# Attention and a routed feed-forward block on one core: the attention half written out without loops, in another order

## The chip, the core and the metric

One NeuronCore of a Trainium2 chip. TensorE (PE) multiplies matrices into PSUM, VectorE (DVE), ScalarE (ACT) and GpSimd (POOL) work on tiles in SBUF and PSUM, SyncE (SP) issues the DMAs. Each engine runs its own instruction list in order; the lists are tied together by semaphores. The metric is the time of one execution on the device in microseconds (us), less is better.

## The reference

x has 32 sequences of 256 tokens of width 128. One layer, two halves:

```python
x = x + attention(layernorm(x))      # 16 heads of 8, scale 1/sqrt(8)
#   allowed = (j <= i) & (j >= i - 128); softmax; out @ w_out.T + b_out
x = x + ffn(layernorm(x))            # 16 experts of 64, the best 4 of each token
#   (from the 2 best of 4 groups), silu(g) * u, weights * 2.5, and a shared expert
```

All in float32; the result is 32 x 256 x 128.

## The kernel before

The work goes in 16 steps of 512 tokens (two sequences, b = 0 and 1). Attention runs over all 16 steps and stores its result x1 in a scratch in DRAM; then the feed-forward half runs over 16 steps. In the attention half two steps are in flight: while step i is *prepared*, the step before it is *attended*.

Preparing (all names are functions of one engine's list): POOL and DVE make the LayerNorm (`statistics`, `layer_norm`), PE transposes it (`transpose_x`), ACT takes it out (`xT`); PE projects Q, K and V (`project_qk`, `project_v`). ACT rounds Q and K to float16 (`high_part`), DVE makes the remainder (`low_part`) and a spread form of Q (`qdiag`); SP stores both parts to DRAM and loads them back in another layout (`qstack`, `kstack`). ACT spreads V (`spread_v`). For the softmax a bound of each row is needed: `score_maxima(i, u)`, u = 0 to 7, computes rough scores on PE into two PSUM banks, DVE reduces them (`chunk_maxima`, `row_maxima`, four u per sequence), and SP takes these maxima through DRAM into `qstack` (`load_max`).

Attending: `scores(i, u)`, u = 0 to 9, five per sequence, writes two PSUM banks `ps_sc`; ACT takes the exponentials (`exps`) and PE may write the next scores when both are done. `attend` and `attend_tails` multiply by V, ACT takes the result (`take_att`), then `transpose_att` (PE), `normalise` (DVE), `transpose_attn` (PE), `take_attn` (ACT), `project_att` (PE) and `add_residual` (DVE) follow one another, for each of the two sequences. POOL's `residual` makes xres for it.

At the end of a body stand the tails, transpositions and projection of sequence 1, and the last maxima; the next body begins with `scores(i, 0)`, which waits for the loaded stacks and maxima. `last` attends step 15 while the weights of the feed-forward half are transposed.

Of the kernel before, what the change touches and what calls it, by code (L numbers as in the profile page):

```python
# [49 lines left out]
def build_block(nc, x, w_in, b_in, w_out, b_out, gate_w, e_bias, gate_proj, up_proj, down_proj,  # L50
# [39 lines left out]
    hl_d = nc.dram_tensor("qk_scratch", [2, P, 2, 2, TOK], FP16).ap()  # L90
# [3 lines left out]
    with ctx:  # L94
# [39 lines left out]
        qstack = [sb(f"qstack{p}", [P, G, TOK], FP16) for p in range(2)]  # L134
        kstack = [sb(f"kstack{p}", [P, G, TOK], FP16) for p in range(2)]
# [92 lines left out]
        w_loaded = sem("w_loaded")  # L228
        const_ready = sem("const_ready")
# [116 lines left out]

        @block.sync
        def _(sp):
            for p in range(2):
                sp.sem_inc(x1_stored[p], 16)  # L350
                sp.sem_inc(stored[p], 16)
# [3 lines left out]
            for n in range(2):  # L355
                sp.dma_start(bqk[:, n:n + 1], b_in[n * P:(n + 1) * P].unsqueeze(1)).then_inc(w_loaded, 16)
            sp.dma_start(bv[:, :], b_in[2 * P:3 * P].unsqueeze(1)).then_inc(w_loaded, 16)
            sp.dma_start(boB[:, :], b_out.partition_broadcast(P)).then_inc(w_loaded, 16)
            sp.dma_start(xin[1][:, :, :], x_t[1]).then_inc(x_loaded[1], 16)
            gu = wgu_raw[:, :, :]  # L360
            for n, w in enumerate((gate_proj, up_proj)):
                sp.dma_start(gu[:, n * NP:(n + 1) * NP, :],
                             w.rearrange("e i h -> (e i) h").rearrange("(n p) h -> p n h", p=P)).then_inc(ffn_loaded, 16)
            sp.dma_start(wsh_raw[0:I, :], sh_gate).then_inc(ffn_loaded, 16)
            sp.dma_start(wsh_raw[I:2 * I, :], sh_up).then_inc(ffn_loaded, 16)
            sp.dma_start(wr_raw[:, :], gate_w).then_inc(ffn_loaded, 16)
            sp.dma_start(wd_raw[:, :, :], down_proj.rearrange("e h i -> h e i")).then_inc(ffn_loaded, 16)
            sp.dma_start(wds_raw[:, :], sh_down).then_inc(ffn_loaded, 16)
            sp.dma_start(bias[:, :], e_bias.partition_broadcast(P)).then_inc(ffn_loaded, 16)
            sp.wait_ge(buffers_ready, 1)  # L370
# [5 lines left out]
            def store_split(i):  # L376

                p = i.parity

                if i.begun:  # L380
                    sp.wait_ge(sc_full, i.lag(2 * UNITS, 0))
                sp.sem_inc(sp_passed, 1)
                for part, ready in ((0, high_ready), (1, low_ready)):
                    sp.wait_ge(ready, i.count(2, 2))
                    sp.dma_start(hl_d[p, :, part], hl[:, part, :, :]).then_inc(split_stored[p], 16)
                sp.wait_ge(split_stored[p], i.half(32, 32))
                for stack, n, parts in ((qstack[p], 0, (0, 1, 0)), (kstack[p], 1, (0, 0, 1))):
                    for t, part in enumerate(parts):
                        for r in range(C):
                            sp.dma_start(stack[32 * r + HD * t:32 * r + HD * t + HD, :, :],  # L390
                                         hl_d[p, :, part, n, :].rearrange("(g r d) t -> r d g t", g=G, r=C)[r]
                                         ).then_inc(qk_loaded[p], 16)

            def load_max(i, b):

                if i.begun:
                    sp.wait_ge(max_loaded[b], i.count(16, 0))
                sp.sem_inc(sp_passed, 1)
                sp.wait_ge(rowmax_ready, i.count(2, b + 1))
                sp.dma_start(mx_d[b], rowmaxT[b][:, :]).then_inc(max_stored[b], 16)  # L400
                sp.wait_ge(max_stored[b], i.count(16, 16))
                sp.dma_start(qstack[i.parity][3 * HD:P:32, :, b * S:(b + 1) * S],
                             mx_d[b].rearrange("(c g n) q -> c g (n q)", c=C, g=G)
                             ).then_inc(max_loaded[b], 16)

            def load_x(i):
                src = x_t[row(i, 2)]
                sp.wait_ge(xres_ready, i.count(1, 1))
                sp.dma_start(xin[i.parity][:, :, :], src).then_inc(x_loaded[i.parity], 16)

            def store_x1(i):

                p = 1 - i.parity
                dst = x1_d[row(i, -1)]
                sp.wait_ge(x1_ready, i.lag(2, 2))
                sp.dma_start(dst, x1[p].rearrange("p t e -> p (t e)")).then_inc(x1_stored[p], 16)

            def first(i):
                store_split(i)
                load_x(i)  # L420
                for b in range(2):
                    load_max(i, b)
# [8 lines left out]

            def body(i):
                store_split(i)
                if not (i.j is None and i.c + 2 >= STEPS):
                    load_x(i)
                else:

                    sp.wait_ge(xres_ready, i.count(1, 1))
                    load_x1(Step(None, 0), i.c + 2 - STEPS)
                for b in range(2):  # L440
# [1202 lines left out]
```

## Time and profile before

| | |
|---|---|
| median of 3 runs | 1018.19 us (1014.93 to 1023.9) |
| profiled execution | 1021.8 us, its span 1019.8 us |
| busy PE / DVE / ACT / POOL | 840.5 / 594.7 / 368.4 / 169.6 us |
| mean granted clock of PE | 0.857 of full |
| attention half, to about | 622 us |
| DMA queue of SP | 54768 packets, 44.51 MB |
| queue of instructions | 78 packets, 1.28 MB |

The page shows the span in 40 slices; up to the 24th PE is 6 to 8 tenths busy at a clock of 6 to 9 tenths, after that 9 and 9. In the rows below, a row of the order of time gives start, duration, engine, line, operation, what is written from what is read, and in brackets the idle time of that engine before it with what ended it; neighbouring instructions of one kind are merged (x8).

### The profile page before, as it was taken

To read this page: it belongs to the slowest core of one execution; us is meant where nothing else is said; L and a number is where in the kernel's file an instruction comes from. 1 tells how busy PE (TensorE), PEld (TensorE's weight loads), DVE (VectorE), ACT (ScalarE), POOL (GpSimd) and SP (SyncE) were. 2 spreads that over 40 slices of the span, in tenths; PEclk is the share of its full clock that TensorE was granted. 3 is DMA by queue.
4 is the path that set the end of the run, shared out by engine and by line. 5 is a ranking of instruction groups with operands and counts; after the bars stand their busy time and mean duration, and the time that the engine had idled before them with its cause. 6 is when DMAs were issued, how large, how long until landed. Compare 5 with 4: busy or idle time off the path is not lost. (4 is left out here: it accounts for less than half of the span.)

```text
span 1019.8 us, 25253 instructions
## 1 busy us (share of the span) xinstructions
PE 840.5 (82%) x8978; PEld 525.6 (52%) x9009; DVE 594.7 (58%) x1874; ACT 368.4 (36%) x709; POOL 169.6 (17%) x289
## 2 busy tenths in 40 slices
PE   3677787777686786777777778999999999999998
PEld 2454444444354453444544446656666666666665
DVE  6545445454554454464455436777777777777774
ACT  2234434343442443444345262332323332323332
POOL 5401101100110110111011102222121222222200
PEclk9667776797797787797768777999999999999999
DMA  4323123213313412331132101110110110100000
GB/s 126 67 36 76 46 32 75 54 54 46 72 42 40 75 54 36 64 69 46 38 76 55 33 1 52 32 31 31 31 31 31 31 31 31 31 31 31 21 21 21
DMA packets 54859, 45.88 MB, mean 45 GB/s; under 512 B 12513, under 2 KB 44529, under 8 KB 54769
## 3 DMA queue, kind: packets, MB, share of 16 engines
q1 hardware_dynamic: 54768, 44.51, 19.9%
q8 instruction: 78, 1.28, 0.6%
q14 instruction: 13, 0.10, 0.0%
HBM read 27.44 MB, written 17.04 MB: 44 GB/s over the span
## 5 line engine op out<-in xcount | busy, mean ns | idle before, releaser
L687 ACT ACTIVATE probs<-ps_sc 128x512 f32<-128x512 f32 x256 | 139.0, 595 | 155.3 <-PE ps_sc L1280 155.2
L868 DVE TENSOR_REDUCE chunkmax<-ps_max 128x16 f32<-128x512 f32 (+1 forms) x256 | 155.0, 647 | 62.5 <-PE ps_max L1244 62.5
L766 ACT ACTIVATE spare<-ps_max 128x512 f32<-128x512 f32 x144 | 85.9, 597 | 212.3 <-PE ps_max L1515 171.2
L1262 PE MATMUL ps_max<-hl,qdiag 32*128 32x160 f16 (+4 forms) x1024 | 59.7, 248 | 84.6 <-DVE chunkmax L868 80.3
L1531 PE MATMUL ps_c<-spare,wd 128*128 128x512 f32 x256 | 125.4, 592 | 0.0
L1302 PE MATMUL ps_sc<-qstack,kstack 32*64 32x192 f16 (+2 forms) x2048 | 75.5, 263 | 44.5 <-ACT probs L687 23.6
L1326 PE MATMUL ps_att<-probs,vdiag 128*32 128x192 f32 (+1 forms) x1536 | 96.6, 403 | 4.8 <-ACT probs L687 4.7
L1092 DVE TENSOR_TENSOR spare<-spare,ps_sc 128x512 f32<-128x512 f32 x128 | 87.2, 681 | 21.7 <-ACT spare L766 11.7
L1262 PEld LDWEIGHTS ps_max<-hl,qdiag 32*128 32x128 f16 x1024 | 39.2, 107 | 111.5 <-DVE chunkmax L868 96.4
L1100 DVE TENSOR_TENSOR spare<-spare,ps_att 128x512 f32<-128x512 f32 x128 | 87.2, 681 | 10.7 <-PE ps_att L1523 4.1
L1302 PEld LDWEIGHTS ps_sc<-qstack,kstack 32*64 32x64 f16 x2048 | 42.4, 120 | 88.3 <-ACT probs L687 43.5
L1513 PE MATMUL ps_max<-xh,whigh 128*128 128x512 f32 x144 | 79.4, 552 | 0.1
L554 POOL TENSOR_TENSOR xres<-xin,cvec 128x512 f32<-128x512 f32 x16 | 20.8, 1298 | 347.1 <-DVE x L914 343.3
L902 DVE RECIPROCAL rden<-ps_b 128x32 f32<-128x32 f32 x32 | 11.4, 358 | 114.9 <-PE ps_b L1356 114.9
L1326 PEld LDWEIGHTS ps_att<-probs,vdiag 128*32 128x32 f32 x1536 | 54.6, 137 | 32.1 <-issue 7.4
L528 POOL TENSOR_TENSOR veps<-meanvar,eps 128x4 f32<-128x4 f32 x32 | 7.6, 236 | 326.2 <-DVE meanvar L841 326.2
L1531 PEld LDWEIGHTS ps_c<-spare,wd 128*128 128x128 f32 x256 | 48.4, 189 | 23.7 <-issue 11.5
L1280 PE MATMUL ps_sc<-edges,repeat 64*128 64x192 bf16 (+2 forms) x576 | 57.5, 276 | 0.0
L1515 PE MATMUL ps_max<-xh,wlow 128*128 128x512 f32 x144 | 57.5, 399 | 0.0
L1514 PE MATMUL ps_max<-xl,whigh 128*128 128x512 f32 x144 | 57.2, 397 | 0.0
L698 ACT COPY attTn<-ps_c 128x256 f32<-128x256 f32 x32 | 11.9, 372 | 123.1 <-PE ps_c L1364 123.1
L914 DVE TENSOR_TENSOR x<-ps_c,xres 128x256 f32<-128x256 f32 x32 | 13.6, 425 | 67.5 <-PE ps_c L1370 67.5
(156 smaller groups left out, 1430.3 us busy)
## 6 DMA issues: line engine op xcount, KB each, us to landing
qk_scratch<-hl SPq DMA_DIRECT2D x32, 256.0 KB, 2.3
qstack<-qk_scratch SPq DMA_DIRECT2D x192, 32.0 KB
kstack<-qk_scratch SPq DMA_DIRECT2D x192, 32.0 KB
xin<-in_L_attn_x_dram SPq DMA_DIRECT2D x16, 256.0 KB, 5.4
x_scratch<-x SPq DMA_DIRECT2D x16, 256.0 KB, 2.7
xin<-x_scratch SPq DMA_DIRECT2D x16, 256.0 KB, 3.0
xres<-x_scratch SPq DMA_DIRECT2D x16, 256.0 KB, 2.7
out_dram<-result SPq DMA_DIRECT2D x16, 256.0 KB, 2.5
```

What stands on the lines that cost most here:

```text
L687: nc.scalar.activation(dst[:, :], ps_sc[s][:, 0:dst.shape[1]], ACT.Exp, scale=SCALE).then_inc(probs_ready, 1)
L766: nc.scalar.activation(silu[slot][rows, :], ps_max[slot][rows, :], ACT.Silu).then_inc(silu_ready, 1)
L868: nc.vector.tensor_reduce(chunkmax[:, 2 * pair + m, at:at + CHUNKS[h]], ps_max[m][:, 0:BANK_COLS[h]].rearrange("p (n k) -> p n k", k=KB), ...
L1092: tt(gated[slot][:, :], silu[slot][:, :], ps_sc[slot][:, :], ALU.mult).then_inc(gated_ready, 1)
L1100: tt(inter[p % 3][:, :], gated[(k.parity + p) % 2][:, :], ps_att[:, :], ALU.mult).then_inc(inter_ready, 1)
L1262: mm(ps_max[m][:, at:at + width], qdiag[rows, b * NB + n, :, :].rearrange("p c k -> p (c k)"), hl[rows, 0, 1, b * S + key0:b * S + key0 + ...
L1280: return mm(ps_sc[s][:, cols].rearrange("p (n k) -> p n k", n=n), repeat2[rows, :, :].rearrange("p e k -> p (e k)"), edges2[rows, edge, :] ...
L1302: mm(dst, kstack[p][rows, jj, q0:q0 + TB], qstack[p][rows, jj, q0:q0 + QCOLS[m]].rearrange("p (n k) -> p n k", k=TB), start=(at == 0), sto ...
L1326: last = mm(ps_att[32 * x:32 * x + 32, half * S + TB * m:half * S + TB * m + QCOLS[m]].rearrange("p (n k) -> p n k", k=TB), vdiag[p][:, (b ...
L1513: mm(bank[slot][:, :], whigh[:, n, :], xh[q][:, :], start=True, stop=False)
L1515: last = mm(bank[slot][:, :], wlow[:, n, :], xh[q][:, :], start=False, stop=True)
L1531: last = mm(ps_c[:, :], wd[:, p, :], inter[p % 3][:, :], start=(p == 0), stop=False)
```

## The change

The whole attention half is written out for all 16 steps (the feed-forward half keeps its loops). A body i now attends `now = i - 1` and prepares `prep = i`, and three things cross its seam: the second sequence of the step before (`transpose_att(now - 1, 1)`, `normalise`, `transpose_attn`, `project_att`, `add_residual`) runs between the first scores of the next body, and so do the eighth `score_maxima` and the second `row_maxima` of the step just prepared. V is projected by four matmuls, each of 128 tokens by all 128 columns, and `spread_v` picks the 64-token halves out with four copies. Q and K lie in one tile `qkstack`; the DRAM scratch has the layout of the stacks, so it is stored with 8 DMAs and loaded with 12. In the prologue, the weights, the small biases and the output bias have a semaphore each, the zeroing of the buffers of parity 1 comes later, and the feed-forward weights are loaded at the end of body 1.

```diff
-    hl_d = nc.dram_tensor("qk_scratch", [2, P, 2, 2, TOK], FP16).ap()
+    hl_d = nc.dram_tensor("qk_scratch", [2, 32, 4, G, TOK], FP16).ap()
...
 # SP
+            for i in BODIES:
+                load_max(i - 1, 1)
+                store_x1(i - 2)
+                load_x(i + 1)
                 store_split(i)
+                load_stacks(i)
+                load_max(i, 0)
+                if i == 1:
+                    load_ffn_weights()
...
+                    for g in range(G):
+                        sp.dma_start(hl_d[p][:, part::2, g, :], hl[32 * g:32 * g + 32, part, :, :]
+                                     ).then_inc(split_stored[p], 16)
...
+                    for t, parts in enumerate((slice(0, 4, 2), slice(0, 4, 3), slice(1, 3, 1))):
+                        rows = slice(32 * r + HD * t, 32 * r + HD * t + HD)
+                        sp.dma_start(qkstack[p][rows, :, :, :], src[r][:, parts, :, :]).then_inc(qk_loaded[p], 16)
...
 # POOL
+            for i in range(STEPS):
+                residual(i)
+                layer_norm(Step(None, i + 1))
+                if i == 0:
+                    other_constants()
...
 # ACT
+                now, prep = i - 1, i
+                exps(now, 0)
+                take_attn(now - 1, 1)
+                exps(now, 1)
+                high_part(prep, 0)
+                exps(now, 2)
+                high_part(prep, 1)
+                exps(now, 3)
+                exps(now, 4)
+                spread_v(prep)
+                exps(now, 5)
+                take_att(now, 0)
+                exps(now, 6)
+                exps(now, 7)
+                take_attn(now, 0)
+                exps(now, 8)
+                exps(now, 9)
+                transpose_out(prep + 1)
+                take_att(now, 1)
...
 # PE
-                for n in range(part * NKB // 2, (part + 1) * NKB // 2):
-                    for e in range(2):
-                        last = mm(ps_a[TB * e:TB * e + TB, n * TB:(n + 1) * TB].rearrange("p (n d) -> p n d", d=HD),
-                                  xT[:, n * TB:(n + 1) * TB], wv[:, e], start=True, stop=True,
-                                  tile_position=(0, TB * e))
+                mm(ps_a[:, t * P:(t + 1) * P], xT[:, t * P:(t + 1) * P], wT[:, 2, :], start=True, stop=True
+                   ).then_inc(v_done, 1)
...
+                now, prep = i - 1, i
+                scores(now, 0)
+                transpose_att(now - 1, 1)
+                project_v(prep, 0)
+                score_maxima(now, 7)
+                scores(now, 1)
+                transpose_attn(now - 1, 1)
+                project_qk(prep, 0)
+                project_att(now - 1, 1)
+                scores(now, 2)
+                project_v(prep, 3)
+                project_qk(prep, 1)
+                scores(now, 3)
+                project_v(prep, 1)
...
+                score_maxima(prep, 0)
+                attend(now, 0, 0)
+                scores(now, 4)
+                project_v(prep, 2)
+                score_maxima(prep, 1)
+                scores(now, 5)
+                attend(now, 0, 1)
+                score_maxima(prep, 2)
+                attend_tails(now, 0)
+                scores(now, 6)
+                transpose_att(now, 0)
+                score_maxima(prep, 3)
+                scores(now, 7)
+                transpose_attn(now, 0)
+                attend(now, 1, 0)
+                scores(now, 8)
+                score_maxima(prep, 4)
+                transpose_x(prep + 1)
+                project_att(now, 0)
+                scores(now, 9)
+                score_maxima(prep, 5)
+                attend(now, 1, 1)
+                attend_tails(now, 1)
+                score_maxima(prep, 6)
```

TensorE at the seam of two steps. Before, inside the loop body (L1342 is `attend_tails`, L1262 and L1244 the maxima, L1356 `transpose_att`, L1364 `transpose_attn`, L1370 `project_att`, L1302 and L1280 the scores, L1218 Q and K):

```order
L1342 MATMUL ps_att<-tails,vdiag 32x64 x8
...
L1356 MATMUL ps_b<-ident,attT 128x128 x4
L1226 MATMUL ps_a<-wT,xT 64x64 x4
L1364 MATMUL ps_c<-ident,att 128x128 x2
L1370 MATMUL ps_c<-wT,attTn 128x128 x2
```

After (L1391 the tails, L1305 and L1286 the maxima, L1347 and L1323 the scores, L1408, L1422, L1432 the three pieces of sequence 1, L1271 a piece of V, L1264 Q and K):

```order
L1391 MATMUL ps_att<-tails,vdiag 32x64 x8
...
L1347 MATMUL ps_sc<-qkstack 64x3x64 x8
...
L1408 MATMUL ps_b<-ident,attT 128x128 x4
L1271 MATMUL ps_a<-wT,xT 128x128
...
L1347 MATMUL ps_sc<-qkstack 64x3x64 x8
...
L1422 MATMUL ps_c<-ident,att 128x128 x2
L1264 MATMUL ps_b<-xT,wT 128x512
L1432 MATMUL ps_c<-wT,attTn 128x128 x2
L1347 MATMUL ps_sc<-qkstack 64x3x64 x8
```

The three pieces that followed one another directly now have scores, maxima or a projection between them.

VectorE around the row maxima of sequence 0. Before (L868 `chunk_maxima`, L902 and L905 `normalise`, L885 to L896 `row_maxima`):

```order
L868 TENSOR_REDUCE chunkmax<-ps_max 128x14
L902 RECIPROCAL rden<-ps_b 128x32
L905 TENSOR_TENSOR att<-ps_b,rden 128x256
L885 TENSOR_REDUCE rowmax<-chunkmax 128x4x3
L885 TENSOR_REDUCE rowmax<-chunkmax 128x4 x5
```

After (L897, L934 and L937, L916 to L926):

```order
L897 TENSOR_REDUCE chunkmax<-ps_max 128x16 x2
L934 RECIPROCAL rden<-ps_b 128x32
L937 TENSOR_TENSOR att<-ps_b,rden 128x256
L897 TENSOR_REDUCE chunkmax<-ps_max 128x14 x2
L916 TENSOR_REDUCE rowmax<-chunkmax 128x4x3
L916 TENSOR_REDUCE rowmax<-chunkmax 128x4 x5
```

`normalise` stood with the row maxima behind the fourth pair of reductions; now it stands in front of that pair.

SP in one step. Before (L385 the split, L390 the stacks, L409 x, L400 and L402 the maxima, L416 x1):

```order
L385 DMA qk_scratch<-hl 128x1024 x2
L390 DMA qstack<-qk_scratch 8x4x512 x12
L390 DMA kstack<-qk_scratch 8x4x512 x12
L409 DMA xin<-in_L_attn_x_dram 128x4x128
L400 DMA max_scratch<-rowmaxT 128x32
L402 DMA qstack<-max_scratch 4x4x256
```

After, the same operations of a step (L419 and L421 the maxima, L442 x1, L432 x, L397 the split, L411 the stacks, in all 12):

```order
L419 DMA max_scratch<-rowmaxT 128x32
L421 DMA qkstack<-max_scratch 4x4x256
L442 DMA x_scratch<-x_0 128x512
L432 DMA xin<-in_L_attn_x_dram 128x4x128
L397 DMA qk_scratch<-hl 64x1x512 x8
L411 DMA qkstack<-qk_scratch 8x2x2048 x2
L411 DMA qkstack<-qk_scratch 8x4096
```

The maxima of sequence 1, x1 and x come ahead of the split and the stacks, and those are other pieces: 8 stores and 12 loads.

## Rows read from the trace of the kernel before

**Rows 1.** Windows: span, busy us (instructions) per engine, PE clock, DMA share, GB/s.

```profile
39.50:578.00 538.50, 406.06 (x6942) 250.02 (x6944) 266.32 (x773) 219.16 (x434) 67.24 (x74) 0.78 0.28 54
...
626.10:1019.80 393.70, 382.56 (x1479) 240.16 (x1507) 283.09 (x961) 120.85 (x221) 74.91 (x146) 1.00 0.09 28
...
284.80:300.00 15.20, 13.14 (x242) 8.39 (x240) 8.72 (x26) 8.74 (x17) 1.30 (x1) 1.00 0.07 22
...
312.10:322.30 10.20, 9.97 (x129) 6.21 (x133) 2.83 (x6) 3.75 (x8) 0.00 (x0) 0.50 0.43 50
...
303.60:312.00 8.40, 4.90 (x133) 3.16 (x128) 5.13 (x16) 3.52 (x8) 0.33 (x1) 1.00 0.47 70
```

**Rows 2.** Order of time: first scores of the first and of the sixteenth step.

```profile
39.52 0.64 PE L1302 MATMUL ps_sc<-qstack,kstack 32*64 32x192 f16 x12
...
577.96 0.41 PE L1302 MATMUL ps_sc<-qstack,kstack 32*64 32x192 f16 x12
```

**Rows 3.** TensorE's waits in the 15 steps: total us, times, longest.

```profile
PE ps_max L1262 <- DVE chunkmax L868: 69.1, 45, 3.1
...
PE ps_sc L1302 <- issue: 19.8, 6, 3.6
```

**Rows 4.** Order of time: the two kinds of 3 us holes on TensorE.

```profile
312.21 0.55 PE L1262 MATMUL ps_max<-hl,qdiag 32*128 32x160 f16 x8 [3.04 <-DVE chunkmax L868]
...
330.38 0.64 PE L1302 MATMUL ps_sc<-qstack,kstack 32*64 32x192 f16 x12 [3.06 <-issue]
```

**Rows 5.** Order of time, TensorE alone, a stretch at full clock.

```profile
288.33 1.08 PE L1326 MATMUL ps_att<-probs,vdiag 128*32 128x192 f32 x24
...
289.33 0.45 PE L1226 MATMUL ps_a<-wT,xT 128*64 128x64 f32 x8
...
289.72 0.43 PE L1342 MATMUL ps_att<-tails,vdiag 128*32 128x64 f32 x16
...
290.46 0.37 PE L1262 MATMUL ps_max<-hl,qdiag 32*128 32x160 f16 x8
...
290.86 0.66 PE L1356 MATMUL ps_b<-ident,attT 128*128 128x128 f32 x4
...
291.44 0.45 PE L1226 MATMUL ps_a<-wT,xT 128*64 128x64 f32 x8
...
293.96 0.41 PE L1302 MATMUL ps_sc<-qstack,kstack 32*64 32x192 f16 x12
...
294.64 1.10 PE L1218 MATMUL ps_b<-xT,wT 128*128 128x512 f32 x2
...
296.53 0.41 PE L1302 MATMUL ps_sc<-qstack,kstack 32*64 32x192 f16 x12
```

**Rows 6.** Order of time: one round of scores and exponentials.

```profile
306.10 0.41 PE L1302 MATMUL ps_sc<-qstack,kstack 32*64 32x192 f16 x12
...
306.79 1.08 ACT L687 ACTIVATE probs<-ps_sc 128x512 f32<-128x512 f32 x2 [1.69 <-PE ps_sc L1280]
...
307.93 0.41 PE L1302 MATMUL ps_sc<-qstack,kstack 32*64 32x192 f16 x12 [0.37 <-ACT probs L687]
```

**Rows 7.** Order of time: the spreading of Q beside POOL, and without it.

```profile
17.20 2.17 DVE L855 TENSOR_SCALAR qdiag<-hl,headrow 128x512 f16<-128x512 f16 x4
...
17.37 1.33 POOL L554 TENSOR_TENSOR xres<-xin,cvec 128x512 f32<-128x512 f32 x1 [3.51 <-DVE cvec L934]
...
334.17 1.14 DVE L855 TENSOR_SCALAR qdiag<-hl,headrow 128x512 f16<-128x512 f16 x4 [4.72 <-ACT hl L666]
```

**Rows 8.** Order of time: twelve load issues on SP.

```profile
303.69 4.07 SPq L390 DMA_DIRECT2D qstack<-qk_scratch  x12
```

**Rows 9.** SP's waits over the span: total us, times, longest.

```profile
SPq L402 <- DMA max_scratch<-rowmaxT: 67.0, 32, 5.1
```

**Rows 10.** Order of time: prologue, the load that held SP, the weight transposes.

```profile
6.16 4.19 SPq L364 DMA_DIRECT2D wsh_raw<-L_ffn_shared_gate_w_dram  x1
...
8.99 1.11 PE L1380 MATMUL ps_b<-ident,wraw 128*128 128x128 f32 x4 [8.99 <-DMA boB<-in_L_attn_b_out_dram]
```

More of the change, by code:

```diff
@@ L344, in steps, with after, valid @@
             last(Step(None, STEPS))
+        def after(engine, semaphore, value):
+            if value > 0:
+                engine.wait_ge(semaphore, value)
+        def valid(d, last=STEPS - 1):
+            return 0 <= d <= last
+        BODIES = range(-1, STEPS + 2)
         @block.sync
@@ L424, in load_x1 @@
+            for p in range(2):
+                sp.wait_ge(x1_stored[p], 16 * (STEPS // 2))
             def load_x1(k, d):
@@ L574, in _, with other_constants @@
             pool.wait_ge(cvec_ready, 1)
[L576 to L581 removed]
+            def other_constants():
                 nc.gpsimd.memset(repeat2[:, :, :], 0.0).then_inc(const_ready, 1)
@@ new lines, in body @@
+            def body(i):
+                now, prep = i - 1, i
+                normalise(now - 1, 1)
+                chunk_maxima(now, 7)
+                row_maxima(now, 1)
+                add_residual(now - 1, 1)
+                spread_q(prep)
+                low_part(prep, 0)
+                low_part(prep, 1)
+                chunk_maxima(prep, 0)
+                chunk_maxima(prep, 1)
+                statistics(Step(None, prep + 1))
+                chunk_maxima(prep, 2)
+                normalise(now, 0)
+                chunk_maxima(prep, 3)
+                row_maxima(prep, 0)
+                if i == 0:
+                    clear(1)
+                chunk_maxima(prep, 4)
+                chunk_maxima(prep, 5)
+                add_residual(now, 0)
+                chunk_maxima(prep, 6)
@@ L1115, in add_y, with last @@
                                         xres[p][:, :, :], ALU.add).then_inc(result_ready, 1)
-            def last(i):
+            def last(now):
                 k = Step(None, 0)
+                normalise(now - 1, 1)
+                chunk_maxima(now, 7)
+                row_maxima(now, 1)
+                add_residual(now - 1, 1)
                 dve.wait_ge(ffn_loaded, 16 * 8)
@@ L1541, in transpose_y, with last @@
                 last.then_inc(y_tr_done, 1)
-            def last(i):
+            def last(now):
+                scores(now, 0)
+                transpose_att(now - 1, 1)
+                score_maxima(now, 7)
+                scores(now, 1)
+                transpose_attn(now - 1, 1)
+                project_att(now - 1, 1)
+                scores(now, 2)
                 pe.wait_ge(ffn_loaded, 16 * 8)
```

650 lines of the change are left out of this document (285 added, 365 removed).

## Prediction

> **What bounds the kernel now.** I read the stretches first, then the waits of TensorE, then one stretch in order of time, always asking which wait ends last.
>
> The feed-forward half, from 626.1 us on, has TensorE 97% busy at a clock of 1.00 [rows 1]. The change does not touch it, so it stays, 394 us. The attention half is where everything is decided: from the first `scores` (39.52 us) to the first `scores` of `last` (577.96 us) lie 15 steps [rows 2], 538.4 / 15 = 35.9 us each. In them TensorE is busy 406 of 538 us, at a mean clock of 0.78; VectorE is busy 266 / 15 = 17.8 us a step and ScalarE 219 / 15 = 14.6 us [rows 1]. No engine is full. Three things fill the step:
>
> - Waits of TensorE for `chunkmax`, 69.1 us in all, and "issue" waits of 3.1 us at the loop's back edge, 19.8 us in 6 [rows 3]. One row of each is in [rows 4]: the `score_maxima` behind row maxima and normalisation on VectorE (3.04 us), and `scores(i, 0)` after the branch (3.06 us); in the seam inside the loop body, where no branch is, that wait does not occur (the `scores` at 293.96 in [rows 5] begins without one).
> - The clock. A clock of 0.78 made of 1.0 and 0.5 means 44% of the stretch at 1.2 GHz, 237 us. The stretch after the 3 us wait, 312.10 to 322.30, runs at 0.50 with TensorE 9.97 of 10.20 us busy; 284.80 to 300.00, with only short waits, runs at 1.00 [rows 1]. So a 3 us hole costs itself and then a stretch at half level, in which TensorE is the bound.
> - The serial end of a step: tails, `transpose_att`, normalise, `transpose_attn`, copy, `project_att` with no scores between them; from `attend` at 288.33 to the next scores at 293.96 pass 5.6 us [rows 5] in which the exponentials stand still.
>
> **The change, part by part.** The sum is made against the profiled execution, 1021.8 us; the median shown is 1018.2.
>
> *TensorE's work in a step at full level*, start to start in [rows 5]: four `attend` at 1.00, eight `score_maxima` at 0.40, `transpose_att` 0.58 twice, Q and K projections 1.89 together, eight full `scores` up to 0.68 and two short ones (estimate 0.46), tails 0.43 twice as durations, the value projection 4 x 0.39, and for the transposes of x, of the normalised heads and the output projections 0.6, 2 x 0.4 and 2 x 0.65 (estimates from the four transposes at 0.58). Sum 21.7 us. The 128-token value matmuls: 16 that stream 64 columns become 4 that stream 128, half as many columns in all. Bounds: no gain (1.6 us) and half of it (0.8 us); I take 1.2, nearest to four pieces like a transpose and its load. So 21.3 us of TensorE at full level; at half level twice that, 42 us.
>
> *ScalarE's chain.* One pair of exponentials takes 1.08 us and the whole round scores, exponentials, next scores takes 1.83 us (306.10 to 307.93) [rows 6]. Eight rounds of 1.83 and two short ones of 1.3 (estimate) are 17.2 us. Of ScalarE's 14.6 us a step about 10 are exponentials; the other 4.6 (`take_attn`, `high_part`, `spread_v`, the copies) partly fall into its waits for scores and partly lengthen a round; I add 3, so about 20.5 us. `spread_v` becomes four copies of half the size for two: under 0.5 us more, inside those 3.
>
> *VectorE.* The same instructions, 17.8 us, plus short semaphore waits: 19 to 20 us. New order: the last `chunk_maxima` and `row_maxima` of a step move behind the seam, `normalise` between two maxima, and between maxima 3 and 4 TensorE now has scores 7, scores 8 and a whole `attend` (about 2.4 us) to do while VectorE makes the row maxima. That is the cover of the old 3.04 us hole; I leave 0.5 us of it.
>
> *The seam.* `transpose_att`, `transpose_attn` and `project_att` of half 1 now stand between scores 0, 1 and 2 of the next step, and each latency to VectorE or ScalarE is covered by a scores piece. 5.6 us shrink to the 2.2 us of TensorE work that is in them. Following all four engines through one body at these durations I get about 21 to 21.5 us: every engine nearly full, TensorE first.
>
> *What is added on top.* (1) `residual` is released by `add_residual(now-1, 1)` and now runs beside `spread_q`. In the prologue of the kernel before those two overlap and `qdiag` takes 2.17 us for its four pieces; alone it takes 1.14 [rows 7]. Cost 0 to 1.0 us a step, I take 1.0, VectorE having no slack. The Trainium skill (SBUF — State Buffer, Who interferes with whom) says that a VectorE operation in a two-port mode and a GpSimd one exclude each other for the whole instruction; by it the full 1.0 is paid, against this change, as I took it. (2) SP: the split is stored in 8 issues for 2, loaded in 12 for 24. Twelve issues take 4.07 us [rows 8], 0.34 each, so 20 issues cost 6.8 us for 8.8 before. With the last `low_part` at about 8 us into the body, stores land at 13, load issues end at 17, row maxima (ready at about 17) go out then and come back behind the loads at 21 to 22, when scores 0 wants them. The bound from below is nothing; from above the worst wait of L402 before, 5.1 us for the store, against its mean of 67.0 / 32 = 2.1 [rows 9]. I take 0.7 us. (3) Some stretches at half level remain after holes, in the hardest places (after scores 5 and at the seam). Bounds: none, and as much as now. 10 us at half level do 5 us of work; I take 1.5 us a step, 3 us at half level in 24.5.
>
> Step after: 21.3 + 1.0 + 0.7 + 1.5 = **24.5 us**, gain 11.4 a step, 15 x 11.4 = **171 us**. The back edges' 19.8 us are inside it.
>
> *Once.* Prologue: the weight transposes waited for the last bias load, until 8.99 us [rows 10]; their own two loads are among the first three issued, so they can go some 3 us earlier, but the LayerNorm of x bounds the next piece: between 0 and -6, I take -4. The feed-forward weights' loads, one of which held SP for 4.19 us [rows 10], move from the prologue into body 1, ahead of row maxima, x load and split stores of step 2: between 0 and +12, I take +5. The last part gets half 1 of step 14 and the eighth maxima: +2 to +4, I take +3. Together +4.
>
> 1021.8 - 171 + 4 = 854.8 in a profiled execution; its 3.6 us above the median are half undone: **853 us**.
>
> **The rivals.**
>
> *A. The DMA chain sets the step (0.25).* If stores of 1 KB pieces and loads are no quicker in landing than before, the chain low part, store, load, row maxima, scores 0 takes about 28 us: loads issued from 14, landed at 25 (the 768 KB came in at 70 GB/s, so over 11 us, before [rows 1]), maxima there at 28. Then, with the holes' half-level stretches, 28 to 31 us a step: 1021.8 - 15 x 7.9 + 4 = 907, up to 952. For it: the chain is linear and starts late; against it: the loads are half as many, with longer pieces. The Trainium skill (DMA: Bandwidth & Descriptors, Why a DMA increments its semaphore by 16 and not by 1) says that a copy spreads over the largest number of engines up to 16 that divides its outer dimension: 8 rows would use 8 engines, before and after. By that alone the loads gain nothing but their piece length; no row here shows the engine numbers.
>
> *B. Everything fits (0.10).* No collision, no half level: 21.5 us, 1021.8 - 216 + 4 = 810.
>
> *C. The straight program starves TensorE (0.04), slower.* The loop is gone, 15 bodies are fetched in sequence. A step has (6942 + 6944) / 15 = 926 TensorE instructions; if fetching stalled like the back edge (3.06 us [rows 4]) after every 200 of them, 5 times a step, a step would be 24.5 + 15.3 = 39.8 us: 1021.8 + 15 x 3.9 + 4 = 1084. From four stalls a step on it loses. Against it: inside a loop body of two steps, 284.80 to 300.00 ran 242 matmuls at full level [rows 1], with no such wait. The Trainium skill (Runtime: NRT & Kernel Launch, Instruction fetch mechanics) says that sequential fetch is autonomous and only a taken branch stalls it; by it C does not happen.
>
> *D. Most of the gain is given back (0.06).* Small holes everywhere keep the clock at its present 0.78: TensorE needs 21.3 / 0.78 = 27 us plus the holes of today without the two big kinds, about 33 to 35: 982 to 1012.
>
> The forecast itself: 0.55.
>
> **Numbers.** 853 us. The forecast's own range, with period 23 to 26.5: 830 to 885. To leave out no more than 2 in 10 the range takes in most of A and half of B: 815 to 945. What a measurement tells from no change is about 1%. Faster by over 1%: forecast, A, B and nearly all of D, 0.94; within 1%: 0.02; slower: 0.04.
>
> **What would show it.** In the profile after: attention ending near 460 us and not 622; TensorE 85% or more busy there, clock 0.93 or more; no issue wait of 3 us before `scores`; waits for `chunkmax` under 20 us in all; `qdiag` at twice its mean; TensorE's wait for `max_loaded` before scores 0 under 1 us. A wait of several us there says A, a clock below 0.85 with many small waits D, issue waits inside a body C. I am wrong if VectorE or ScalarE hold a chain that the walk through one body missed.

## The result, and the profile after

The changed kernel takes **949.71 us** (median of 4 runs, 948.31 to 956.55) against 1017.39 of the kernel before beside it: ratio 0.934, 95% interval 0.928 to 0.940. It is faster, as forecast, but the forecast was 853 us and its range ended at 945. The profiled execution took 948.31 us, its span is 946.6. In what follows a ratio rests on fast runs alone, which leaves out one run of e2 (1683.42 us) and two of e2b (886.69 and 885.51).

Windows of the changed kernel (columns as in [rows 1]): the 15 steps and the last part, the feed-forward half, one body while TensorE works, the hole behind it (a stretch in which TensorE does nothing), and the start of the next body.

```profile
36.11:546.60 510.49, 376.87 (x6976) 251.50 (x6972) 291.56 (x850) 239.96 (x502) 73.81 (x85) 0.81 0.28 61
546.60:946.60 400.00, 388.60 (x1504) 244.68 (x1532) 287.02 (x970) 124.95 (x228) 74.92 (x146) 0.99 0.10 30
292.00:315.00 23.00, 22.65 (x440) 15.25 (x440) 17.19 (x51) 14.68 (x31) 4.67 (x5) 0.89 0.29 67
314.90:323.60 8.70, 0.00 (x0) 0.01 (x1) 1.29 (x2) 0.11 (x1) 0.00 (x0) 0.65 0.32 47
...
323.60:329.60 6.00, 5.98 (x58) 3.95 (x59) 2.91 (x12) 2.35 (x5) 0.00 (x0) 0.50 0.01 3
```

The body itself is as dense as hoped: 22.65 of 23.00 us busy. Then TensorE does nothing for 8.7 us, and the next body begins at half level. First scores of the first and of the sixteenth step, against [rows 2]:

```profile
36.11 0.64 PE L1347 MATMUL ps_sc<-qkstack 32*64 32x192 f16 x12
...
506.92 0.64 PE L1347 MATMUL ps_sc<-qkstack 32*64 32x192 f16 x12 [8.96 <-issue]
```

(506.92 - 36.11) / 15 = **31.4 us a step**, for 35.9 before and 24.5 forecast. TensorE's waits over the span, against [rows 3]:

```profile
PE ps_sc L1347 <- issue: 119.3, 15, 9.6
PE ps_max L1305 <- DVE chunkmax L897: 13.3, 6, 6.4
```

The waits for `chunkmax` are nearly gone (69.1 to 13.3). One new wait has come, once a step, 119.3 / 15 = 8.0 us. "issue" names no releaser, so who ended it has to be read from the neighbours. SP's queue through this body, in order of time, gives it:

```profile
297.40 0.34 SPq L419 DMA_DIRECT2D max_scratch<-rowmaxT  x1
298.82 0.54 SPq L421 DMA_DIRECT2D qkstack<-max_scratch  x1
299.41 0.45 SPq L442 DMA_DIRECT2D x_scratch<-x  x1
299.89 0.43 SPq L432 DMA_DIRECT2D xin<-in_L_attn_x_dram  x1
300.94 5.54 SPq L397 DMA_DIRECT2D qk_scratch<-hl  x8
309.01 6.29 SPq L411 DMA_DIRECT2D qkstack<-qk_scratch  x12
315.41 0.35 SPq L419 DMA_DIRECT2D max_scratch<-rowmaxT  x1
321.56 0.54 SPq L421 DMA_DIRECT2D qkstack<-max_scratch  x1
```

And TensorE and VectorE at its two ends:

```profile
310.51 0.21 DVE L926 STREAM_TRANSPOSE rowmaxT<-rowmax 128x32 f16<-128x32 f16 x1
```

```profile
314.62 0.26 PE L1286 MATMUL ps_max<-edges,repeat 32*128 32x192 bf16 x4
323.62 0.64 PE L1347 MATMUL ps_sc<-qkstack 32*64 32x192 f16 x12 [8.74 <-issue]
```

The row maxima are ready at 310.7. SP is still issuing the 12 stack loads and takes them up at 315.41, just when TensorE runs out of work. Their 8 KB store, which comes back in 1.4 us when it is alone (297.40 to 298.82), now comes back after 6.15 us (315.41 to 321.56), behind 768 KB of stack loads in the same queue. Their load leaves then, and 2.06 us later scores 0 starts. The windows behind the last load issue (315.30) show what the store waited for: the stack loads' data were still moving, until 320.0.

```profile
315.30:320.00 4.70, 0.00 (x0) 0.00 (x0) 0.90 (x2) 0.00 (x0) 0.00 (x0) 0.74 0.52 77
320.00:321.50 1.50, 0.00 (x0) 0.00 (x0) 0.00 (x0) 0.00 (x0) 0.00 (x0) 0.50 0.02 1
```

So the loads take 6.29 us to issue, but 11.0 us until their data are in (309.01 to 320.0; 768 KB, about 70 GB/s). SP's waits over the span fit (before: 67.0 in [rows 9]):

```profile
SPq L421 <- DMA max_scratch<-rowmaxT: 97.4, 32, 6.1
```

### The profile page after: what moved, and what is told of

The parts are those of the page before. It is cut to its first block and busy times, and to the rows that moved or that the text cites. A ratio compares the mean times of both kernels' runs of the same rounds, so it can differ in the third digit from the quotient of the medians.

```text
span 946.6 us, 23269 instructions
## 1 busy us (share of the span) xinstructions
PE 778.6 (82%) x8594; PEld 505.3 (53%) x8625; DVE 602.4 (64%) x1874; ACT 371.0 (39%) x741; POOL 170.3 (18%) x289
## 5 line engine op out<-in xcount | busy, mean ns | idle before, releaser
L897 DVE TENSOR_REDUCE chunkmax<-ps_max 128x16 f32<-128x512 f32 (+1 forms) x256 | 155.5, 649 | 38.3 <-PE ps_max L1286 38.2
L1347 PE MATMUL ps_sc<-qkstack 32*64 32x192 f16 (+2 forms) x2048 | 71.7, 252 | 121.7 <-issue 119.3
L1347 PEld LDWEIGHTS ps_sc<-qkstack 32*64 32x64 f16 x2048 | 41.0, 114 | 154.1 <-issue 129.8
L934 DVE RECIPROCAL rden<-ps_b 128x32 f32<-128x32 f32 x32 | 11.4, 357 | 137.4 <-PE ps_b L1408 137.3
L1373 PE MATMUL ps_att<-probs,vdiag 128*32 128x192 f32 (+1 forms) x1536 | 70.6, 318 | 0.0
L1305 PE MATMUL ps_max<-hl,qdiag 32*128 32x160 f16 (+4 forms) x1024 | 53.1, 227 | 15.3 <-DVE chunkmax L897 13.3
L1323 PE MATMUL ps_sc<-edges,repeat 64*128 64x192 bf16 (+2 forms) x576 | 54.1, 262 | 0.0
L1305 PEld LDWEIGHTS ps_max<-hl,qdiag 32*128 32x128 f16 x1024 | 34.2, 98 | 35.9 <-DVE chunkmax L897 20.6
L1373 PEld LDWEIGHTS ps_att<-probs,vdiag 128*32 128x32 f32 x1536 | 44.0, 111 | 16.2 <-issue 3.2
L1552 PE MATMUL ps_sc<-xl,whigh 128*128 128x512 f32 x128 | 51.0, 398 | 0.0
L1553 PE MATMUL ps_sc<-xh,wlow 128*128 128x512 f32 x128 | 50.5, 395 | 0.0
```

Of the source, the lines that this page charges most:

```text
L897: nc.vector.tensor_reduce(chunkmax[:, 2 * pair + m, at:at + CHUNKS[h]], ps_max[m][:, 0:BANK_COLS[h]].rearrange("p (n k) -> p n k", k=KB), ...
L1305: mm(ps_max[m][:, at:at + width], qdiag[rows, b * NB + n, :, :].rearrange("p c k -> p (c k)"), hl[rows, 0, 1, b * S + key0:b * S + key0 + ...
L1347: mm(dst, qkstack[p][rows, 1, jj, q0:q0 + TB], qkstack[p][rows, 0, jj, q0:q0 + QCOLS[m]].rearrange("p (n k) -> p n k", k=TB), start=(at == ...
L1373: last = mm(ps_att[32 * x:32 * x + 32, half * S + TB * m:half * S + TB * m + QCOLS[m]].rearrange("p (n k) -> p n k", k=TB), vdiag[p][:, (b ...
L1552: mm(bank[slot][:, :], whigh[:, n, :], xl[q][:, :], start=False, stop=False)
L1553: last = mm(bank[slot][:, :], wlow[:, n, :], xh[q][:, :], start=False, stop=True)
```

## The experiments

All ratios are against the kernel before on the same chip. "Step" is (first scores of step 15 - first scores of step 0) / 15, read from each trace as above.

### Is it the stack loads, and what about them?

**e1**: 3 loads in place of 12. The rows of a stack are interleaved, so that one DMA brings all 32 rows of a kind, 256 KB.

```diff
-                for r in range(C):
-                    for t, parts in enumerate((slice(0, 4, 2), slice(0, 4, 3), slice(1, 3, 1))):
-                        rows = slice(32 * r + HD * t, 32 * r + HD * t + HD)
-                        sp.dma_start(qkstack[p][rows, :, :, :], src[r][:, parts, :, :]).then_inc(qk_loaded[p], 16)
+                for t, parts in enumerate((slice(0, 4, 2), slice(0, 4, 3), slice(1, 3, 1))):
+                    sp.dma_start(qkstack[p][t:P:4, :, :, :], hl_d[p][:, parts, :, :]).then_inc(qk_loaded[p], 16)
```

> The kernel after, but the 32 rows of a row group of the stacks are interleaved (row 32r + 4d + t instead of 32r + 8t + d), so that one load can fill every fourth of the 128 rows: 3 loads of 32 rows (256 KB each) for 12 of 8 rows. Same data, same result. In the kernel after, TensorE ends its body 23 us after it began and then waits 8.0 us on average for stacks and maxima. Theory W (the loads of 8 rows are slow in themselves, 768 KB in some 9.5 us, and everything behind them waits): data in about 5 us, first scores 5 to 7 us earlier a step, 949.7 - 15 x 6 = 860 (840 to 875). Rival I (what counts is only the time that SP issues, 6.3 us for 12 loads): issue falls to under 2 us, gain about 4 us a step, 890. Rival Q (the maxima's own round trip through DRAM is the long part): gain under 2 us a step, 920 to 950.

**e2**: the interleaved rows, but still 12 loads of 8 rows (`slice(32 * r + t, 32 * r + 32, 4)`).

> As e1_wide_loads in the rows' layout (every fourth row), but still 12 loads of 8 rows. It separates what the eight rows of a load lie next to from how many there are. Theory W by number of rows: no change against the kernel after, 940 to 955. If writing eight neighbouring rows were the slow part: 860 to 900. Rival I and Q: no change.

**e3**: the maxima's store and load issued by GpSimd, ahead of and behind its LayerNorm, instead of by SP.

> The kernel after, but the store and the load of the row maxima are issued by GpSimd and not by SP, so they do not stand behind SP's 12 stack loads. Theory W: the stacks themselves land about 19.5 us after their body's high part, some 3 us before the maxima do now, so the wait of TensorE shrinks from 8.0 to about 4.5 to 5.5 us and not further: 949.7 - 15 x 3 = 905 (890 to 925). Rival Q: the wait goes nearly, 840 to 860. Against both: a GpSimd that is late with the LayerNorm of the next step, because it waits for the store, would make it no faster, 945 or more.

e1: **846.92 us**, ratio 0.832 (0.827 to 0.837), step 24.50. e2: 932.37 (median of the three), 0.913 (0.909 to 0.916), step 30.41. e3: 925.61, 0.907 (0.904 to 0.910), step 29.83. TensorE's wait before the scores in e1, and its SP queue in one body:

```profile
PE ps_sc L1344 <- issue: 32.6, 15, 3.8
```

```profile
266.86 5.48 SPq L397 DMA_DIRECT2D qk_scratch<-hl  x8
273.97 1.87 SPq L408 DMA_DIRECT2D qkstack<-qk_scratch  x3
276.70 0.32 SPq L416 DMA_DIRECT2D max_scratch<-rowmaxT  x1
279.87 0.56 SPq L418 DMA_DIRECT2D qkstack<-max_scratch  x1
```

The same 768 KB in three DMAs, and the wait falls from 8.0 to 2.2 us a step: the loads are the cause of most of it. e1 lies in the range of its theory W. In e3, just over the range of its theory W, the maxima pass the loads by, and TensorE still waits, now for the stacks themselves, with a releaser named:

```profile
PE ps_sc L1348 <- DMA qkstack<-qk_scratch: 83.3, 14, 8.1
```

So the maxima's detour behind the loads is the smaller share: 31.4 - 29.8 = 1.6 us a step (the prologue of e3 is 4 us longer).

Two readings of e1 were left: it has fewer loads, and wider ones (32 rows). **e7** parts them: 12 loads of 32 rows, 64 KB each.

```diff
+                for t, xs in enumerate(((0, 2), (0, 3), (1, 2))):
+                    for n, x in enumerate(xs):
+                        for g in (0, 2):
+                            sp.dma_start(qkstack[p][t:P:4, n, g:g + 2, :], hl_d[p][:, x, g:g + 2, :]).then_inc(qk_loaded[p], 16)
```

> As e1_wide_loads, 32 rows in each load, but 12 loads of 64 KB (pieces of 2 KB) for 3 of 256 KB: the same number and size of loads as in the kernel after. Theory W (the number of rows in a load is what counts): data in some 5 us, SP's issue time of about 6 us is then the longer part, 855 to 880. Rival I (12 issues are what makes it slow): 935 to 955, as after and e2_spread_rows.

**e2b**: 6 loads of 16 rows.

> The change with 6 stack loads of 16 rows and 4 KB a row instead of 12 of 8 rows (between e1, 3 loads of 32 rows, and e2 and e7, 12 loads of either 8 or 32 rows). Theory I (SyncE pays for each load by number, up to 0.7 us an issue): issue time near the straight line between 1.9 us for 3 and 8.5 us for 12, so about 4.1 us for 6; TensorE's wait before the first scores 2 us longer than e1's 2.2, step near 26.5 us, time 865 to 885. Rival theory W (rows and engines in a load decide, with 32 rows as the good case): 16 rows lie near 8 rows' 8 us of wait, 905 to 930. Rival S (only the first few issues are cheap, a queue's depth of some 6 to 8 outstanding loads has to be filled first): 6 still cost little, 845 to 855.

e7: 933.85, 0.915 (0.911 to 0.920), step 30.25. e2b: 881.01 and 868.20, against 1017.99 (no interval was formed), step 26.79 in the first of them, which was profiled. The loads' issue in each:

```profile
295.68 8.46 SPq L410 DMA_DIRECT2D qkstack<-qk_scratch  x12
```

```profile
295.60 4.19 SPq L410 DMA_DIRECT2D qkstack<-qk_scratch  x6
```

My theory W, that the rows of a load decide, fell: 12 loads of 32 rows (933.85) are as slow as 12 of 8 rows four apart (e2, 932.37). So e1's time lay in W's range for another reason. With the rows interleaved the number of loads decides, through the issue: 3, 6 and 12 loads (e1, e2b, e7) take 1.87, 4.19 and 8.46 us of SP, 0.62 to 0.71 us each, and give steps of 24.5, 26.8 and 30.3 us, 0.76 and 0.58 us of the step for each load more. A load costs 0.70 us in six as in twelve, against rival S of e2b.

The changed kernel itself is another case, and its 12 loads of 8 neighbouring rows must not be put in that row. They issue in 6.29 us, faster than e7's, but their data go on for 4.7 us behind the last issue, at a DMA share of 0.52. In e2 (first line) and e7 (second) the data end 1.3 us behind the last issue:

```profile
306.86:308.20 1.34, 0.00 (x0) 0.00 (x0) 0.00 (x0) 0.00 (x0) 0.00 (x0) 0.73 0.36 101
304.14:305.50 1.36, 0.00 (x0) 0.00 (x0) 0.00 (x0) 0.00 (x0) 0.00 (x0) 0.59 0.46 105
```

From the first load issue to the last data are 11.0 us in the changed kernel, 9.8 in e2 and e7, and 4.5 in e1 (273.97 to 278.5). What ends this time is the moving of the data in the first and the issuing in e2 and e7; nearly equal steps hide two limits. Why eight neighbouring rows move more slowly than eight rows four apart is open.

**e8** made the same loads wide in the kernel before (6 for 24):

> The kernel before with the interleaved rows and 6 loads of 32 rows for 24 of 8. There no wait of TensorE for stacks or maxima is in the trace, so the loads have slack: no change, 1012 to 1022, if the reading is right that the slow loads were hidden in steps of 36 us and only the short step of the new order uncovers them. If they already cost something there: under 1010.

1018.33 against 1018.67, ratio 0.999 (0.996 to 1.002). There the loads were covered, as expected; it is the change that puts them on the path.

### What is left in e1?

**e5**: e1 with `residual` behind the LayerNorm on GpSimd, so that it no longer meets `spread_q`.

> e1_wide_loads, with GpSimd's residual behind the LayerNorm of the next step and no longer in front of it, so that it does not run beside the spreading of Q on VectorE. In e1 the four pieces of qdiag take 578 ns each in the steps, 349 in the kernel before. Theory C (VectorE waits out GpSimd, and it has no slack): qdiag back to 349, 0.9 us a step, 847 - 14 = 833 (830 to 840). Theory N (VectorE has slack there): qdiag back to 349 and the time unchanged, 843 to 851.

847.59, 0.831 (0.828 to 0.834): no gain. By line and form, busy us and mean ns, of e1 and then of e5 (both 36 to 405 us), and then of the kernel before (39.5 to 578 us):

```profile
L872 DVE TENSOR_SCALAR qdiag<-hl,headrow 128x512 f16<-128x512 f16 x60 | 31.1, 578 | 2.4 <-ACT hl L677 2.4
L919 DVE TENSOR_SCALAR rowmax<-rowmax 128x32 f16<-128x32 f32 x30 | 5.4, 181 | 1.0
```

```profile
L875 DVE TENSOR_SCALAR qdiag<-hl,headrow 128x512 f16<-128x512 f16 x60 | 17.1, 348 | 1.9 <-ACT hl L680 1.7
L922 DVE TENSOR_SCALAR rowmax<-rowmax 128x32 f16<-128x32 f32 x30 | 16.0, 532 | 1.0
```

```profile
L855 DVE TENSOR_SCALAR qdiag<-hl,headrow 128x512 f16<-128x512 f16 x60 | 17.1, 349 | 37.7 <-ACT hl L666 37.7
L891 DVE TENSOR_SCALAR rowmax<-rowmax 128x32 f16<-128x32 f32 x29 | 15.2, 524 | 1.0
```

`qdiag` was freed (578 to 348 ns), but another operation met GpSimd instead (`rowmax`, 181 to 532 ns), so VectorE gained only 36.5 - 33.1 = 3.4 us in 15 steps, and e5 is no test of what the collision costs. The kernel before had the same collision at `rowmax` (524 ns): the change moved it to `qdiag` and added 36.5 - 32.3 = 4.2 us, 0.3 a step. The Trainium skill (SBUF — State Buffer, Who interferes with whom) calls the shared port an exclusive lock; the trace agrees with these lengths. What the collision costs at most is seen in e13b below, where `qdiag` still takes 562 ns and TensorE is 96% busy.

**e10**: e1 with the old value projection (16 matmuls of 64 by 64, two copies), to price the new one.

> e1_wide_loads with the value projection of before: 16 matmuls of 64 columns and two spreading copies for 4 of 128 columns and four copies. It prices that part of the change. The prediction took 0.4 us a step from TensorE, 6 us in all: 853 (848 to 860). If TensorE does not set the step there: 845 to 850; if the two copies fewer on ScalarE count more: under 845.

861.24, 0.843 (0.839 to 0.848), step 25.43 for 24.50, just over the expected range: the new projection with its copies is worth 0.9 us a step there.

**e11**: e1 with 2 split stores of 128 rows in place of 8 of 32, into the same scratch layout. **e1p** and **e12**: e1 and e11 with the maxima issued by GpSimd.

```diff
-                    for g in range(G):
-                        sp.dma_start(hl_d[p][:, part::2, g, :], hl[32 * g:32 * g + 32, part, :, :]
-                                     ).then_inc(split_stored[p], 16)
+                    sp.dma_start(hl_d[p][:, part::2, :, :].rearrange("r x g t -> g r x t"), hl[:, part, :, :]
+                                 ).then_inc(split_stored[p], 16)
```

> e1 (3 wide stack loads) with 2 split stores of all 128 rows in place of 8 of 32 rows; same bytes and same pieces of 1 KB. Theory I (cost by the number of DMAs): the stores' issue falls from 5.5 us to the 2.4 us that 2 stores took before the change; the loads leave 3 us earlier, TensorE's 2.2 us before the scores go; step 22.3 to 23.0, time 815 to 828. Rival D (issue time goes with the number of pieces in a DMA, not with the number of DMAs): the 2 stores take 5 us too, and the time stays at 845 to 850.

> e1 (3 wide stack loads) with the maxima's store and load issued by GpSimd instead of SyncE. In e1 the store of the second half's maxima leaves at 276.70 and its load at 279.87, 3.17 us later, against 1.4 for the first half's; TensorE waits 2.2 us a step at the first scores. Theory I: what is left of the wait is the maxima's round queued behind the stack loads on SyncE's queue: on another queue the load leaves 1.5 us earlier, the stacks themselves then end the wait; step 23.0 to 24.0, time 825 to 842. Rival: what is left is the chain of 8 split stores (5.5 us) and the stack loads' own landing, so nothing changes, 845 to 852; or GpSimd, in order, stands 3 us in the two rounds ahead of LayerNorm, and the time goes up to 855 to 870.

> e11 with the maxima's rounds issued by GpSimd as well. Theory I: after e11 nothing is left to gain from SyncE's queue but what sits behind the stack loads, within 1% of e11, 812 to 828: TensorE has the bound then, at 21.3 to 22.5 us a step. Rival: GpSimd's own rounds delay LayerNorm and it is 1 to 2% slower than e11.

e11: 876.48, 0.860 (0.858 to 0.863). e1p: 863.09, 0.845 (0.840 to 0.850). e12: 861.25, 0.845 (0.842 to 0.849). All three are slower than e1; both theories of e11 missed, and so did theory I of e1p and e12. Moving the maxima to GpSimd made e1 16 us slower (e1p) and e11 15 us faster (e12). The queue of e11, its waits, and the window in which its stores land:

```profile
287.23 1.67 SPq L396 DMA_DIRECT2D qk_scratch<-hl  x2
296.43 1.86 SPq L407 DMA_DIRECT2D qkstack<-qk_scratch  x3
```

```profile
SPq L405 <- DMA qk_scratch<-hl: 122.1, 16, 8.3
```

```profile
288.90:296.40 7.50, 7.24 (x182) 4.82 (x174) 6.41 (x24) 5.94 (x14) 3.28 (x4) 1.00 0.24 71
```

Issuing fell to 1.67 us as expected, but landing rose to 122.1 / 16 = 7.6 us, at 71 GB/s with a DMA share of 0.24. The store's outer dimension in the scratch is the 4 head groups. The Trainium skill (DMA: Bandwidth & Descriptors, Why a DMA increments its semaphore by 16 and not by 1) says that a DMA runs on the largest number of engines up to 16 that divides the outer dimension of both sides, so on 4 here; a share of 0.24 fits 4 of 16. The rule alone does not tell e2 from the changed kernel, both with 8 rows in a load: the share of 0.52 behind the changed kernel's last issue fits 8 of 16, while in e2, where the issuing is the limit, it is 0.36.

Why e1p lost those 16 us I did not settle. It lies in the range of its rival that GpSimd stands in the maxima's rounds ahead of LayerNorm (855 to 870), but no row shows that. Its first scores come 4.2 us later (40.47 for 36.23), once; TensorE's wait stays mostly an "issue" one.

**e13b** tests the outer dimension of the stores: the scratch laid out by its 128 rows as before the change, 2 stores with those rows outside, and 6 loads of 32 rows in 1 KB pieces (so its loads differ from e11's too). **e15**: e1 with the four high-part stores issued by ScalarE. **e17**: e13b with its high-part store on ScalarE.

```diff
-    hl_d = nc.dram_tensor("qk_scratch", [2, 32, 4, G, TOK], FP16).ap()
+    hl_d = nc.dram_tensor("qk_scratch", [2, P, 4, TOK], FP16).ap()
...
+                    sp.dma_start(hl_d[p][:, part::2, :], hl[:, part, :, :]).then_inc(split_stored[p], 16)
...
+                src = hl_d[p].rearrange("(g r) x t -> r x g t", g=G)
+                for t, xs in enumerate(((0, 2), (0, 3), (1, 2))):
+                    for n, x in enumerate(xs):
+                        sp.dma_start(qkstack[p][t:P:4, n, :, :], src[:, x, :, :]).then_inc(qk_loaded[p], 16)
```

> The change with the scratch laid out by rows as before (128 rows, so 2 split stores of 128 rows each), and 6 stack loads of 32 rows in pieces of 1 KB: 8 DMAs in place of the 20. In e11 2 stores took 1.67 us to issue but 7.5 us to land, with the 4 head groups as the outer of the store. Theory L (landing goes by how many rows the outer of a DMA has): with 128 rows outside the stores land in 2.5 us, the loads leave by 4.5 us after the low part is ready, against 7.2 in e1, and end their issue 0.3 us ahead of e1's: step and time as e1 or a little under, 835 to 850. Rival: the landing of 2 stores is slow because one DMA carries 256 KB, whatever its outer; then they take 7 us here too, 895 to 910.

> e1 (3 wide stack loads) with the 4 stores of the high part issued by ScalarE, right behind the two copies that make it, and the 4 of the low part by SyncE as now. Theory I (the chain is SyncE's time for issuing, and two queues issue side by side): of e1's 5.5 us of store issue 2.7 go from SyncE, so the loads leave 2.2 to 2.7 us earlier and TensorE's 2.2 us before the scores nearly go: 815 to 835. ScalarE gives 2.8 us a step to it, of 24.5 of which 14 are busy; the rival is that this makes TensorE wait at the probabilities instead: 850 to 870.

> e13b with the high part's one store issued by ScalarE and the low part's by SyncE. Theory I and L: the high store is issued and landed before the low part is even ready, so the loads leave 1 us earlier than in e13b, and ScalarE pays 0.7 us: 815 to 840, 0 to 2% under e13b. If the low store's own landing sets the time, the same as e13b within 0.5%.

e13b: **810.05 us**, 0.793 (0.788 to 0.799), better than I had expected (835 to 850), and the best kernel here but for e17's 808.78, 0.792 (0.787 to 0.798), which can't be told from it; so issuing the high part's store elsewhere gains nothing more. The queue of e13b, SP's wait for its stores, TensorE's wait before the scores, and the windows of its first four steps and of the eleven others:

```profile
289.88 1.57 SPq L396 DMA_DIRECT2D qk_scratch<-hl  x2
293.70 4.10 SPq L408 DMA_DIRECT2D qkstack<-qk_scratch  x6
299.58 0.32 SPq L416 DMA_DIRECT2D max_scratch<-rowmaxT  x1
301.07 0.54 SPq L418 DMA_DIRECT2D qkstack<-max_scratch  x1
```

```profile
SPq L404 <- DMA qk_scratch<-hl: 48.6, 16, 4.0
290.50:293.70 3.20, 3.12 (x88) 2.15 (x84) 2.61 (x5) 1.93 (x7) 0.00 (x0) 1.00 0.76 250
```

```profile
PE ps_sc L1344 <- issue: 7.7, 8, 2.4
```

```profile
35.54:131.84 96.30, 88.94 (x1754) 58.55 (x1750) 70.96 (x205) 58.66 (x123) 17.77 (x20) 0.91 0.32 95
131.84:367.83 235.99, 227.01 (x4840) 152.79 (x4837) 200.39 (x573) 161.39 (x341) 50.16 (x55) 1.00 0.30 90
```

With 128 rows outside SP waits 48.6 / 16 = 3.0 us for the 2 stores, for 7.6 in e11. The 250 GB/s of the window are not theirs alone: 3.20 us at that rate are 800 KB, the stores are 512 KB, and x and x1 were issued just before them. From the first store's issue to the first load's pass 3.8 us, against 7.1 in e1, and the whole round to the end of the load issues takes 7.9 us against 9.0 in e1 and 14.4 in the changed kernel (300.94 to 315.30). The maxima now go out in an idle queue and are back in 1.5 us. From step 4 on a step is 235.99 / 11 = **21.5 us**, with TensorE 96% busy at a clock of 1.00: it is the bound, as rival B had it (over all 15 steps the mean is 22.2). Why the first four steps take 24.1 us is open.

e15: 877.11, 0.858 (0.851 to 0.865), above both of its ranges and 30 us slower than e1. SP's issue time fell, ScalarE's rose, and TensorE now waits for the exponentials (0.3 us in e1), as the rival named there; its "issue" wait before the scores fell from 32.6 to 1.3 us. ScalarE's queue and TensorE's wait:

```profile
284.93 2.72 ACTq L688 DMA_DIRECT2D qk_scratch<-hl  x4
287.75 1.08 ACT L715 ACTIVATE probs<-ps_sc 128x512 f32<-128x512 f32 x2 [2.90 <-issue]
```

```profile
PE ps_sc L1356 <- ACT probs L715: 40.8, 24, 3.3
```

One such store costs 0.68 us on either engine (2.72 / 4 on ScalarE, 5.48 / 8 on SP in e1).

### What did the order itself give?

**e4**: the kernel before with its attention loops written out, and nothing else.

> The kernel before, with the attention bodies of all five engines written out (no hardware loop), in the old order and with the old pieces. It prices the loops alone. The 3.1 us waits before scores at the back edges go, 19.8 us in 6, and with each of them some us of half clock: expected 1017 - 20 - 7 x 2 = 983 (970 to 998). A theory that the straight program is fetched too slowly gives 1017 or more.

994.88, ratio 0.978 (0.974 to 0.982), inside the expected range, step 34.01 for 35.90, no back-edge wait left, but the waits for `chunkmax` up (80.3 us over the whole span of the kernel before):

```profile
PE ps_max L1265 <- DVE chunkmax L871: 86.8, 55, 3.3
```

Leaving the loops out gives 1019.49 - 994.88 = 24.6 us, between 18 and 27 by the interval. The rest of the change, the order together with the new projection and the new DMAs, gives the other 45 us to 949.71.

## Why the prediction was wrong

**The step that failed** is term (2) of what is added on top, SP's chain, taken as 0.7 us a step. It cost 8.0 us, 7.3 more. All other terms together came out 0.4 us better, so the step was 6.9 us longer than forecast, 103 us in 15 steps. What happens once came out 7 us better and the feed-forward half 2.6 us, which leaves the 94 us between 948.3 and the forecast 854.8 of a profiled execution. The walk in that term against the trace, from the body's first scores at 291.94 us:

| | forecast, us into the body | measured |
|---|---|---|
| last `low_part` ready | 8 | 10.2 |
| stores landed, loads begin | 13 | 17.1 |
| load issues end | 17 | 23.4 |
| row maxima ready | 17 | 18.8 |
| data of the loads in | no figure | 28.1 |
| maxima back, scores 0 | 21 to 22 | 31.7 |

Three things were mis-sized. First the issue: 0.34 us from [rows 8] for all 20, where a store took 5.54 / 8 = 0.69 and a load 6.29 / 12 = 0.52, 11.8 us for 6.8. The row was of another DMA (8 rows by 4 pieces of 1 KB, 32 KB), and no row of a split store stood beside it: in the kernel before, two of those took 2.37 us to issue (from 298.99 us). Second, the low part was ready 2.2 us later. Third, the walk ended the loads with their last issue and left their landing to rival A. Their data moved for 4.7 us more, and the maxima's store, taken to go round with its load in 4 to 5 us, came back after 6.15 alone, so that scores 0 began 8.3 us behind the last load issue. The upper bound of 5.1 us came from a kernel that had other work there, so it bounded nothing.

- **Rival A** was right, just over its upper end in the step: 31.4 us for its 28 to 31, 949.7 for its 952. It had 0.25. Its price of the landing, 768 KB at 70 GB/s in over 11 us, is what the changed kernel shows (11.0); what it left out is that the loads begin at 17.1 and not at 14. Issuing takes the place of the landing in e2 and e7.
- **TensorE's 21.3 us at full level, and all engines fitting**: right. The body works in 23.0 us at a clock of 0.89; e13b, with the compute engines' order unchanged and only DMAs and scratch layout other, has a step of 21.5 with 227.01 / 11 = 20.6 busy. The old value projection was costed 0.4 us above the new; e10 gives 0.9, over the bound of 0.8.
- **The seam and the chunkmax wait**: right; 69.1 fell to 13.3 us, under the 20 named. TensorE 85% busy and a clock of 0.93 were not met (74% and 0.81), both below because of the hole and the half level behind it.
- **Term (1), the collision**: it happened (2.19 us for four pieces in one body, `qdiag` at 578 ns in e1 for 285 alone), but the term missed that the kernel before paid the same at `rowmax`: the net on VectorE is 0.3 us a step. In e13b `qdiag` is still at 562 ns and only 4% of a step of 21.5 us, 0.9 us, is idle on TensorE, for whatever reason. 1.0 was too much there; what it cost in the changed kernel no run shows.
- **Term (3), half level left, 1.5 us**: in the changed kernel it was about 3 (6.00 us at half level behind the hole do 3.0 us of work); with the chain short it is 0 (clock 1.00 in e13b from step 4 on).
- That e1 landed at 847, near my 853, is then partly chance: its 2.2 us of wait stand where 1.0 of collision and 1.5 of half level were priced.
- **Once**: first scores at 36.11 for 39.52, -3.4 (forecast -4). The last part, from the sixteenth step's scores to the feed-forward half, 39.7 us for 39.2, +0.5 (forecast +3). The feed-forward loads in body 1 cost little: the first two steps take 31.7 and 32.5 us, the mean 31.4 (forecast +5). The feed-forward half, taken as unchanged, is 2.6 us shorter in this execution.
- **Rival C** is refuted: no issue wait inside a body, and e4, equally straight, is faster than its loops. **D** too: no small holes, one large one.

## What to carry to other kernels

When a change shortens the compute of a step, walk the DMA chain again with the number of DMAs on one queue, and price each by a row of the same shape; a chain that was hidden at 36 us a step was the bound at 31. Price the landing as well as the issue, whichever ends last. Here few DMAs with many rows outermost on both sides were best: 8 in place of 20 for the same bytes, with another layout, brought 949.7 to 810.05 us. Look for small transfers that others wait for behind large ones on the same queue: here it cost 1.6 us a step (e3), and the cure by another engine made e1 slower (e1p). And a step that is equally long in two variants need not have the same limit in both.

## What was new of the hardware

- An issue on SP or ScalarE took 0.34 (8 rows, 1 KB pieces), 0.52 (8 neighbouring rows, 4 KB pieces), 0.62 (32 rows, 256 KB) and 0.68 to 0.71 us (8 rows four apart, 16 rows, 32 rows of 64 KB). It does not follow the bytes; what it follows is open.
- Two stores of 256 KB: 71 GB/s with 4 groups outside, and a wait of 7.6 us for them; 3.0 us with 128 rows outside.
- 768 KB in 12 loads of 8 rows: with neighbouring rows 6.29 us of issue and 11.0 until the data are in, with rows four apart 8.45 and 9.8.
- Behind the 8.7 us hole TensorE ran at half level (clock 0.50, 5.98 of 6.00 us busy); in e13b, with TensorE 96% busy, it held 1.00 over 236 us.
